# Bf16 parts in 32-bit words: the middle part read as the upper half of the fp32 rest

## The reference

```python
in_agg = jax.ops.segment_sum(edge_feat, receivers, num_segments=N_NODES)
out_agg = jax.ops.segment_sum(edge_feat, senders, num_segments=N_NODES)
to_updater = jnp.concatenate([in_agg, out_agg, node_feat], axis=1)
h = jax.nn.relu(to_updater @ W1 + b1)
...
x = _layernorm(x + h @ W2 + b2, axis=-1)
```

## Time and profile before

| what | us |
|---|---|
| median of 3 runs | 1480.26 |
| lowest and highest run | 1479.1, 1482.73 |
| profiled execution: its span | 1367.2 |
| median less this span | 113.1 |
| PE busy | 1136.3 (83%) |
| DVE busy | 1180.0 (86%) |
| ACT busy | 986.0 (72%) |
| POOL busy | 1090.7 (80%) |

### The profile page before, as it was taken

How to read it: one execution, slowest core, us unless ns; L and a number is a source line. 1 busy time by engine, 2 the same in 40 slices (tenths; PEclk the granted TensorE clock), 3 DMA queues, 4 the chain that set the end, 5 groups by cost and what they waited for, 6 DMA issues and landing times.

```text
span 1367.2 us, 63623 instructions
## 1 busy us (share of the span) xinstructions
PE 1136.3 (83%) x23123; PEld 964.3 (71%) x23123; DVE 1180.0 (86%) x3631; ACT 986.0 (72%) x2259; POOL 1090.7 (80%) x663
## 2 busy tenths in 40 slices
PE   2666688888888888888888878888988889989796
PEld 2546478778877888787777767777777777777543
DVE  6656689999999899989899989899999899998686
ACT  6233589999999999999899976666666667666332
POOL 3878888888888888888888888888888888888533
PEclk9975899999999999999999999999999999999998
DMA  9332399999999999999999998888988888888641
GB/s 303 44 43 15 34 205 212 222 215 217 213 224 216 211 216 222 215 216 215 224 248 244 240 219 219 211 201 214 228 215 225 213 216 215 199 209 192 134 132 47
DMA packets 262841, 263.21 MB, mean 193 GB/s; under 512 B 106099, under 2 KB 223956, under 8 KB 262486
## 3 DMA queue, kind: packets, MB, share of 16 engines
q1 hardware_dynamic: 170152, 231.66, 55.4%
q0 software_dynamic: 92384, 28.77, 28.1%
q10 hardware_dynamic: 144, 0.52, 0.2%
HBM read 146.90 MB, written 113.96 MB: 191 GB/s over the span
## 4 chain that ended last, share of the span: by engine, by line
PE 31%; DMA 26%; issue 17%; POOL 13%; DVE 8%; ACT 2%; SPq 1%; DVEq 0%; POOLq 0%; ACTq 0%
DMA out_tables<-payload,target 22%; PE psum L1693 17%; POOL out_tables L769 13%; PE psum L1669 3%; DVE to_node L1318 3%; DMA feat<-in_edge_attr 3%; PE psum L1880 2%; PE psum L1645 2%; DVE same L1345 1%; PE psum L1652 1%; DMA slots_in<-slot_tiles 1%; PE psum L1747 1%; PE psum L1835 1%; PE psum L1892 1%; DVE rest L1238 1%
## 5 line engine op out<-in xcount | busy, mean ns | idle before, releaser
L769 POOL DMA_INDIRECT out_tables<-payload,target x628 | 1057.3, 1684 | 213.5 <-issue 174.7
L1669 PE MATMUL psum<-parts,to_slot 128*128 128x194 bf16 x4836 | 465.5, 248 | 86.0 <-ACT slots_out L864 79.4
L1669 PEld LDWEIGHTS psum<-parts,to_slot 128*128 128x128 bf16 x4836 | 401.7, 98 | 117.4 <-ACT slots_out L864 97.5
L864 ACT ACTIVATE slots_out<-psum 128x388 bf16<-128x388 f32 x936 | 385.8, 474 | 49.5 <-PE psum L1669 36.1
L1693 PE MATMUL psum<-to_node,slots_in 64*64 64x286 bf16 x10296 | 352.9, 284 | 51.1 <-issue 42.2
L1693 PEld LDWEIGHTS psum<-to_node,slots_in 64*64 64x64 bf16 x10296 | 303.6, 107 | 89.1 <-issue 57.3
L1279 DVE TENSOR_SCALAR to_slot<-iota_h,slot 128x528 bf16<-128x528 f16 (+1 forms) x936 | 295.9, 364 | 52.3 <-PE psum L1669 52.2
L1318 DVE TENSOR_SCALAR to_node<-iota_h,slot_rel 128x286 bf16<-128x286 f16 x858 | 246.4, 310 | 0.7 <-PE psum L1693 0.5
L1318 DVE TENSOR_SCALAR to_node<-iota_rows,slot_rel 128x286 bf16<-128x286 f16 x572 | 192.0, 336 | 0.0
L939 ACT ACTIVATE to_node<-apart 128x286 bf16<-128x286 bf16 x286 | 117.7, 435 | 66.0 <-PE psum L1693 64.5
L931 ACT ACTIVATE apart<-iota_h,slot_rel 128x286 bf16<-128x286 f16 x286 | 137.2, 524 | 11.2 <-DVE slot_rel L1290 11.2
(11 more groups left out here) (138 smaller groups left out, 912.8 us busy)
## 6 DMA issues: line engine op xcount, KB each, us to landing
slot_tiles<-slots_out SPq DMA_DIRECT2D x156, 388.0 KB
feat<-in_edge_attr SPq DMA_DIRECT2D x195, 256.0 KB
slots_in<-slot_tiles SPq DMA_DIRECT2D x168, 242.5 KB
slots_in<-slot_tiles SPq DMA_DIRECT2D x168, 230.4 KB
slot_tiles<-slots_out SPq DMA_DIRECT2D x78, 291.0 KB
out_tables<-payload,target POOLq DMA_INDIRECT x628
out_tables<-zeros POOLq DMA_DIRECT2D x4, 1600.0 KB
feat<-out_tables SPq DMA_DIRECT2D x48, 128.0 KB, 2.3
```

What stands on the lines that cost most here:

```text
L769: e.indirect_dma_start(out_tab, at, payload[b][:, t, :], None, element_offset=k * TABLE_ROWS * D, compute_op=ALU.add).then_inc(s_tab[k], 16)
L864: e.activation(slots_out[b][:, g:g + n, m, :], ps_share[r % BANKS][:, 0:n * SLOT_W].rearrange("p (g w) -> p g w", w=SLOT_W), ACT.Copy).the ...
L1669: last = e.matmul(ps_share[r % BANKS][:, o:o + SLOT_W], to_slot[m][:, COLUMN_FROM[k] + t * P:COLUMN_FROM[k] + (t + 1) * P], parts[b][:, SH ...
```

## The change

The parts of a chunk now lie in 32-bit words: `words[b]` has 195 fp32 words per column in place of 195 bf16 elements, and `parts[b]` is a view of the upper half of each word. High and low part are written into upper halves. The rest is written in fp32 over the 64 words of the middle part, in each of the two buffers, and its upper half is the middle part as it stands, cut off where it was rounded before. So `split_mid`, its semaphore and ScalarE's pass are gone, and split_lo waits for VectorE's own subtraction (`s_rest`). split_rest no longer waits for `s_lo`, as the rest now has two buffers. Everything that reads or writes parts (PE's streamed operands and weights, ScalarE's high part and nodes, VectorE's two passes) now does so with a step of 4 bytes between 2-byte elements. `tab_sum` moves to `words[0]`.

```diff
-        rest = sb("rest", [P, COLS, D])
-        parts_flat = [sb(f"parts{b}", [P, COLS * (1 + SLOT_W)], bf16) for b in range(2)]
-        parts = [flat[:, :].rearrange("p (c w) -> p c w", c=COLS) for flat in parts_flat]
+        words_flat = [sb(f"words{b}", [P, COLS * (1 + SLOT_W)]) for b in range(2)]
+        words = [flat[:, :].rearrange("p (c w) -> p c w", c=COLS) for flat in words_flat]
+        rest = [w[:, :, 1 + D:1 + 2 * D] for w in words]
+
+        parts = [flat[:, :].bitcast(bf16).rearrange("p (c w k) -> p c w k", c=COLS, k=2)[:, :, :, 1] for flat in words_flat]
...
-        tab_sum = [rest[:, GT * b:GT * (b + 1), :].rearrange("p t d -> p (t d)") for b in range(2)]
+        tab_sum = [words_flat[0][:, GT * D * b:GT * D * (b + 1)] for b in range(2)]
...
-            def split_mid(c, b):
-                e.wait_ge(s_rest, c + 3)
-                e.activation(parts[b][:, :, 1 + D:1 + 2 * D], rest[:, :, :], ACT.Copy).then_inc(s_mid, 1)
...
                 slots(i, s, b, range(0, ROUNDS))
-                split_mid(c + 1, 1 - b)
                 slots(i, s, b, range(ROUNDS, CHUNK_ROUNDS))
...
-                    if ahead and not first_sums and q == 0:
-                        split_mid(c + 1, 1 - b)
...
             def split_rest(c, b):
 
-                if not isinstance(c, int) or c > 0:
-
-                    e.wait_ge(s_lo, c)
                 e.wait_ge(s_hi, c + 1)
-                e.tensor_tensor(rest[:, :, :], feat[b][:, :, :], parts[b][:, :, 1:1 + D],
+                e.tensor_tensor(rest[b], feat[b][:, :, :], parts[b][:, :, 1:1 + D],
                                 ALU.subtract).then_inc(s_rest, 1)
 
             def split_lo(c, b):
-                e.wait_ge(s_mid, c + 1)
-                e.tensor_tensor(parts[b][:, :, 1 + 2 * D:1 + 3 * D], rest[:, :, :],
+                e.wait_ge(s_rest, c + 3)
+                e.tensor_tensor(parts[b][:, :, 1 + 2 * D:1 + 3 * D], rest[b],
                                 parts[b][:, :, 1 + D:1 + 2 * D], ALU.subtract).then_inc(s_lo, 1)
```

More of the change, by code:

```diff
@@ L342, in build @@
         s_rest = sem("s_rest")
-        s_mid = sem("s_mid")
         s_lo = sem("s_lo")
@@ L906, in chunk @@
                         out_of_transposes(turned_at(at))
-                    first_sums = mode.sums and at == 0
-                    if first_sums and q == QUADS - 1:
-                        split_mid(c + 1, 1 - b)
                     if mode is EARLY and (c, q) == (0, 0):
@@ L981, in prologue @@
                 split_hi(pair, 2 * pair, 0)
-                split_mid(2 * pair, 0)
             split_hi(0, 0, 0)
-            split_mid(0, 0)
             code_rows(0, 1)
```

1 line of the change is left out of this document (removed).

## The result

The changed kernel takes **1510.7 us** (median of 4 runs, 1508.82 to 1513.13), the kernel before 1479.68 us on the same chip (4 runs, 1477.28 to 1482.73): ratio 1.0189, 95% interval 1.016 to 1.0218. It is slower by 31 us. The forecast was 1479 us and no change; the time lies inside the range, in the part that the rivals B and C had.

What follows compares the result with a forecast made beforehand. The prediction took a loop of PE and ScalarE waits to set the sharing chunks' period, with POOL and VectorE almost as full. Its terms, 0 - 1 + 0 + 0 + 0 = -1 us, gave 1479 us, range 1463 to 1535.

Steps and rivals of the forecast that it cites:

- B: Rival, slower: PE pays for reading at the 4-byte step; 1509 at a fifth of the bound, 1630 at the whole; chance 13%.
- C: Rival, slower: 2-byte writes at a 4-byte step cost more; ScalarE's 1499 at a quarter of its bound, 1557 at all; chance 11%.
- The removed pass: ScalarE's middle pass, 104.3 us busy: worth 0 in the sharing chunks, where its wait for PE grows instead; 1 us in summing.
- Rival A: Faster: the sharing period follows ScalarE's load; full price 51 us (1428), half of it 1454; chance 10%.
- The high part's write: ScalarE writing 2-byte elements at a 4-byte step, inside the loop 78 times: taken as 0, bounds 0 to +78 us.
- the loop: Sets the sharing period: PE from round 4 to round 10's end, 5.07 us, then ScalarE to its first eviction, 3.14 us.
- VectorE's two passes: Subtraction and low part at a 4-byte step, 1.21 us each: taken as 0, growth to about 0.6 us covered by idle time.
- PE's reads: To_slot products streaming 194 columns at a 4-byte step, 43 in the loop: taken as 0, bound +151 us.
- The spread weights: Window products' weights, 64 columns, loaded at the 4-byte step: taken as 0, +60 us if loads took twice as long.
- The moved wait: VectorE's low part waits for its own subtraction, not ScalarE's pass, and the subtraction's wait for the previous low part goes: 0.
- 113 us around the span: Difference between the 1480.26 us median and the profiled span of 1367.2 us, taken as unchanged by the change.
- Rival D: Slower by little: POOL's scatters stretch where VectorE's passes meet them; 0.1 us a chunk is 8 us (1487); chance 4%.

Runs made afterwards that it cites:

- e1_nomid: The kernel before without ScalarE's middle pass, old contiguous layout, the middle part left at zero: ratio 0.9998.
- e5b_high_close: The changed kernel with the high part written, and read by the subtraction, as adjacent elements (sums wrong): ratio 1.0056 to the kernel before.
- e2_words_mid: The changed kernel's words plus a ScalarE pass of the old size into a scratch tile, for which the low part waits: ratio 1.0214 to the kernel before.
- e12_high_low_close: The changed kernel with both the high and the low part written side by side (sums wrong): ratio 1.0017 to the kernel before.
- e9_even_words: The changed kernel with 196 words per column in place of 195, so parts begin on even words: ratio 1.0187 to the kernel before.
- e4_spread_reads: The kernel before, with PE's to_slot products streaming from a constant tile of zeros at a 4-byte step: ratio 1.0048.
- e13_pass_ahead: The kernel before with an extra 300-element ScalarE pass ahead of the high part in each sharing chunk: ratio 1.0098.
- e15_high_later_only: The kernel before with ScalarE evicting rounds 0 and 1 ahead of the high part, VectorE's order unchanged: ratio 1.0491.
- e0b_before: The kernel before, unchanged, profiled once more, on a chip of the quicker kind: 1387.87 us.
- e3_pass_in_loop: The kernel before with an extra 300-element ScalarE pass right behind the high part of each sharing chunk: ratio 1.0026.

## Why the prediction was wrong

- **The removed pass, 0.** Right. e1_nomid, 0.9998; ScalarE's wait grew to 1.35 us (1.78 in the changed kernel, on the slower kind) where I had 1.49, most of it ahead of round 6 and not behind the four evictions as I had it. Rival A is out.
- **The high part's write, taken 0, bounds 0 to +78 us.** This is the step that failed. I chose the contiguous row as the nearer one "because two elements still lie in each 8 bytes". The run showed 1414 ns for 1073, a third of an ns for each of the 1024 elements, 0.34 us a chunk, 27 us by the prediction's own price. Taking it away (e5b_high_close) gave back 19 us. The bounds held it, at a third of the way up. The path was right on the quicker kind of chip (e2_words_mid: 3.46 us for 3.14 in ScalarE's piece of the loop) and incomplete on the slower, where the cost showed mainly in PE's break and not in the wait for the eviction.
- **VectorE's two passes, 0.** Half right. The subtraction, which reads spread, hardly changed (1218 ns for 1212 on the quicker kind, 1225 for 1224 on the slower); the low part, which writes spread, took 0.16 us more. I had called both covered up to 0.6 us. e12_high_low_close gives the low part some 0.4%, with an interval as wide. The rule on odd words of the Trainium skill (Vector Engine (DVE) Microarchitecture Reference, "Measured stream behaviour on trn2") was refuted as the cause here by e9_even_words.
- **PE's reads, 0, bounds 0 to +151 us.** Nearly right: 2 to 4 ns a product, 7 us alone (e4_spread_reads). The spread weights, 0 with a bound of +60: the 48 window products took 0.98 us for 0.95 (e2_words_mid), 2 us in 78 chunks. The Trainium skill, Advanced Engine Details and Errata, "SBUF Cachelines", gives full performance within one 16-byte line; the trace agrees to within 4%, and at 3.4 us for each ns even that was over the 4.4 us that I called no change.
- **The moved wait, 0.** I followed the low part's wait but not the subtraction's. VectorE took the subtraction with no wait before, right behind the high part: 489.53 + 1.07 = 490.60 and 490.64. That link has no slack, and the prediction, which had both rows, priced only ScalarE's loop. What hangs on it had 1.36 us of slack toward PE's round 6. e13_pass_ahead shows that a start 0.34 us later costs something even so, e15_high_later_only what it costs beyond the slack.
- **113 us around the span, unchanged.** Wrong: 2 us lie there. The profile was of a faster execution than the median. It did no harm to the difference, since the prediction added it to both, but it hid that the rows came from the other kind of chip than the times, where PE has a break that the rows did not show.
- **B and C together.** By their prices, 27 us for the write and 3 ns x 3.4 = 10 us for PE make 37 us; 33 (e2_words_mid) and 31 were measured. The rivals were sized well; the chance was not. I had given the forecast 62% on three terms set to 0 next to bounds of 78, 60 and 151 us, each with only an argument for 0. The range had a slip too: its lower end, 1463 us, is a third of A's price and not the half (1454) that the text names.

**Rival D, POOL, 4%.** Its premise, that nothing moves VectorE against POOL, did not hold. POOL's scatters in the sharing stage grew from 1723 ns (e0b_before) to 1829 (e2_words_mid, same kind) and 2028 (changed kernel), and POOL still has hardly a gap beyond the 0.3 us between two scatters. A scatter of over 2.3 us ends about 0.24 us behind VectorE's `onehot`, as here in the changed kernel (490.97 + 3.04 = 494.01, 493.22 + 0.55 = 493.77):

```profile
490.97 3.04 POOL L770 DMA_INDIRECT out_tables<-payload,target  x1 [0.31 <-issue]
```

```profile
493.22 0.55 DVE L1253 TENSOR_TENSOR onehot<-rel,iota_twice 128x768 bf16<-128x768 bf16 x1
```

Such scatters are 53 in the 54 chunks from 240 to 740 us there, 30 in 58 in e2_words_mid, 4 in 61 in the first profile. That the stretching follows the longer chunk and does not make it is argued, not shown by an experiment: where POOL did stand idle for its targets (e4_spread_reads 50.6 us, e5b_high_close 50.4 us), the chunks took 9.15 and 9.13 us, no less than the 9.11 us of e3_pass_in_loop, where it was full; and the chain that ended last has 0% of POOL in the changed kernel and in e2_words_mid.

**What stays open.** Why 0.34 us behind the high part cost 4 us and not 27 on the slower kind of chip; it was not run on the quicker kind, where the loop's sum fits. What PE waits for in the break, and why it grows when VectorE's subtraction comes later: the comparison for round 6 has slack enough, and in the chunk of the changed kernel shown above VectorE idles again, 0.69 us, before its next comparisons (498.34). The kernel before was never traced on the slower kind. Why a VectorE pass more made the kernel 0.3% faster.

## What to carry to other kernels

A pass removed from an engine that then waits is worth nothing; read the wait behind it first. A cheaper layout is paid by every instruction that writes it: for an access that no row shows, 0 is one end of the bounds and needs a row of its own; here a third of the upper bound of one write, 78 times, was enough. For an operation whose end releases another engine, check both who follows it in its own queue and who waits for its semaphore; a row that starts right where it ends, as at 490.64 in the earlier trace rows, has no slack at that link, and how much the chain has is read at its far end, where another engine uses the result. Before comparing a profile with a time, compare the profiled execution's span with that time.

## What the runs showed of the hardware

- ScalarE writing 1024 bf16 elements from fp32 at a 4-byte step took 1414 ns, contiguous 1061 to 1073 ns (changed kernel, e5b_high_close).
- VectorE's subtraction with a bf16 result took 1369 ns at a 4-byte step and 1213 ns contiguous; reading a bf16 operand at that step cost 1 to 6 ns (1225 against 1224 in e5b_high_close, 1218 in e2_words_mid against 1212 in e0b_before). Beginning each row on an even word did not help (1415 ns).
- PE streaming 194 bf16 elements at a 4-byte step paced at 2 to 4 ns above the 85 ns of contiguous ones.
- GpSimd's scatters of over 2.3 us ended 0.18 to 0.25 us behind VectorE's `onehot` comparison, all 53 of them in the changed kernel and all 30 in e2_words_mid from 240 to 740 us; the shortest scatters took 1.55 us.
- Chips differ by 7 to 8% on this kernel (1383 us and 1480 to 1498 us) at about the same mean clock (0.97). PE's break inside the window products appeared on the slower ones alone. The mean of POOL's scatters does not tell them apart: 1737 ns in e2_words_mid on the quicker kind, 1720 in e4_spread_reads on the slower.
